# A selective scan on one core: its units ordered by channel half, one PSUM accumulator, and a third PSUM slot for the preparing steps alone

## What is computed

```python
xz = LN(x) @ in_w.T                      # only layer 0 normalizes
xr, z = split(xz)
xc = silu(causal_conv4(xr) + cb)
dt, Bm, Cm = split(xc @ xw.T)            # ranks 8, 16, 16
dt = softplus(dt @ dtw.T + dtb)
dA  = exp(dt[..., None] * A)             # (b, t, 256, 16)
dBx = dt[..., None] * Bm[:, :, None, :] * xc[..., None]
h_t = dA_t * h_{t-1} + dBx_t;   y_t = sum_s h_t[:, s] * C_t[s]
out = ((y + xc * D) * silu(z)) @ ow.T
```

## Time and profile before

| | us |
|---|---|
| median of 3 runs (lowest to highest) | 6413.47 (6411.19 to 6418.31) |
| the profiled execution, its own time | 6412.89 |
| its span | 6411.1 |
| span of the scan block, first instruction to the last DVE operation | 1285.1 |
| first scan of unit 0 starts | 89.00 |
| granted TensorE clock, mean of the span | 0.939 |

### The profile page before, as it was taken

One profiled execution on the slowest core, in us unless ns is written; L12 is line 12 of the kernel. 1 busy time (PEld: TensorE's weight loads), 2 busy tenths in 40 slices (PEclk: granted clock), 3 DMA queues, 4 the chain that ended last, 5 costly groups with the idle time before them and its releaser, 6 DMA issues. The chain is left out here.

```text
span 6411.1 us, 72562 instructions
## 1 busy us (share of the span) xinstructions
PE 5480.3 (85%) x25739; PEld 2272.5 (35%) x25776; DVE 4251.4 (66%) x4740; ACT 2491.3 (39%) x2863; POOL 2457.2 (38%) x1151
## 2 busy tenths in 40 slices
PE   5777777749999999999999999937888776777999
PEld 2333333323333334433343343313333211222776
DVE  3676667867776777677767767547666888773221
ACT  4444444213222323232232222223555566666332
POOL 3666666716655565556555555500000000000000
PEclk8988998979999999999999999967999899998999
DMA  2222222211111101011101101011111101000000
GB/s 81 86 97 86 86 93 93 95 38 28 30 25 25 29 19 39 21 28 25 40 19 25 30 22 25 20 38 45 38 37 31 31 21 24 18 11 28 1 1 14
DMA packets 114962, 247.35 MB, mean 39 GB/s; under 512 B 27564, under 2 KB 48308, under 8 KB 114324
## 3 DMA queue, kind: packets, MB, share of 16 engines
q1 hardware_dynamic: 114616, 242.71, 13.4%
HBM read 200.81 MB, written 23.86 MB: 35 GB/s over the span
## 5 line engine op out<-in xcount | busy, mean ns | idle before, releaser
L2097 DVE TENSOR_REDUCE n_MX<-ps 128x2 f32<-128x1024 f32 (+1 forms) x896 | 979.1, 1108 | 289.0 <-PE ps L1860 206.6
L1547 POOL TENSOR_TENSOR s_PA<-s_PA,s_TMP 128x1024 f32<-128x1024 f32 x384 | 906.5, 2361 | 321.7 <-ACT s_TMP L1268 293.3
L1969 ACT ACTIVATE n_P<-ps 128x1024 f32<-128x1024 f32 (+2 forms) x896 | 804.7, 936 | 462.3 <-PE ps L1878 240.9
L1268 ACT ACTIVATE s_TMP<-ps 128x1024 f32<-128x1024 f32 x512 | 523.9, 1025 | 1145.8 <-PE ps L1128 1133.9
L673 POOL TENSOR_TENSOR m_PR<-m_HH,m_CS 128x1024 f32<-128x1024 f32 x256 | 604.7, 2374 | 395.5 <-DVE m_HH L635 164.9
L1399 DVE TENSOR_REDUCE s_MX<-ps 128x2 f32<-128x1024 f32 x512 | 593.1, 1201 | 17.1 <-PE ps L1111 16.6
L1391 DVE TENSOR_TENSOR XTB<-ps,s_GVJ 128x1024 f32<-128x1024 f32 x256 | 312.9, 1222 | 401.5 <-PE ps L1102 399.1
L1124 PE MATMUL ps<-s_QF 64*128 64x512 f32 x2048 | 554.8, 618 | 10.7 <-DMA s_M<-s_MS 8.4
L472 PE MATMUL ps<-m_PR,ident 128*128 128x512 f32 x1024 | 540.8, 662 | 11.8 <-POOL m_PR L673 11.1
L1904 PE MATMUL ps<-n_P,n_VA 128*32 128x512 f32 (+3 forms) x3584 | 523.1, 582 | 12.2 <-ACT n_P L1969 12.2
L1111 PE MATMUL ps<-s_QF 64*128 64x512 f32 x2048 | 497.9, 603 | 32.9 <-DVE XTB L1391 30.6
(11 more groups left out here) (309 smaller groups left out, 7418.6 us busy)
## 6 DMA issues: line engine op xcount, KB each, us to landing
m_CS<-m_rows_c SPq DMA_DIRECT2D x128, 512.0 KB, 3.9
m_BS<-m_rows_c SPq DMA_DIRECT2D x80, 512.0 KB, 4.8
s_WV<-in_s_v SPq DMA_DIRECT2D x32, 512.0 KB, 3.5
s_TA<-XTB SPq DMA_DIRECT2D x256, 64.0 KB, 2.3
s_WO<-in_s_o SPq DMA_DIRECT2D x32, 512.0 KB, 3.9
n_parts<-n_PT SPq DMA_DIRECT2D x16, 768.0 KB, 3.3
n_QS<-n_parts SPq DMA_DIRECT2D x192, 64.0 KB
n_KS<-n_parts SPq DMA_DIRECT2D x192, 64.0 KB
```

Of the source, the lines that this page charges most:

```text
L1268: s.activation(self.P[g % 4], ps, ACT.Exp).then_inc(*r.take(step))
L1547: g.tensor_tensor(PA, PA, P, ALU.add).then_inc(self.add_done, 1)
L1969: s.activation(self.P[(32 * n + 8 * hp + t) % 3][q][:, :, lo:512], ps.rearrange("p (h n) -> p h n", h=2)[:, :, lo:512], ACT.Exp, scale=sca ...
L2097: v.tensor_reduce(self.MX[:, q, :, hp, t], ps.rearrange("p (h n) -> p h n", h=2)[:, :, 0:width], AX.X, ALU.max).then_inc(*r.take(step))
```

## The change

1. A unit is now `h = m // 16 % 2`, `j = m % 16`: 16 units of half 0, then 16 of half 1. Each unit loads its own C row (`c_in` 256 times instead of 128).
2. There is one accumulator, `PY` (two banks). The first `sum` of a half waits until the half before it is gated. So `gate(n, 0)` stands behind unit 18 and `gate(n, 1)` behind unit 2 of the next item.
3. The two banks that come free are slot 2, which only the side steps use. Units keep slots 0 and 1.
4. Side steps stand at written-out places (`sides`), and the reader's part of a step is a step of its own (`..._t`), one unit or so behind its PE part. The two long `in` are cut in halves (`in0`, `in`) with unit steps between. `dt`, `ln` and `soft` of half 1 are made in the item itself (units 5 to 8) and those of half 0 in the item before (22 to 26); `ln` is done half by half.
5. `make(m + 1)` now comes before `exp(m + 3)`; C is asked for 3 units ahead, B 5. `m_PR` has four tiles instead of three; DT and U have one copy, not two; `m_T` is its own tile.
6. The statistics of all four sequences' layernorms are taken in the first stretch (`stats`, `others`), and later `norm` is only the 8 scalings. The weights for the first matmuls are loaded first, and PE waits for each weight only where it uses it.

```diff
-        self.PY = [PS[:, 0:1024], PS[:, 1024:2048]]
-        self.r = Ring(nc, ctx, "m_psum", [PS[:, 2048:3072], PS[:, 3072:4096]],
+        self.PY = PS[:, 0:1024]
+        self.r = Ring(nc, ctx, "m_psum", [PS[:, 1024:2048], PS[:, 2048:3072], PS[:, 3072:4096]],
...
+    SIDE = 2
+    def sides(self, n):
+        at = {}
+        if n > 0:
+            at[2] = [("gate", n - 1, 1)]
+            at[3], at[4] = [("post", n - 1)], [("post_t", n - 1)]
+        at[5], at[6] = [("dt", n, 1)], [("dt_t", n, 1), ("ln", n, 1)]
+        at[7], at[8] = [("soft", n, 1)], [("soft_t", n, 1)]
+        at[18] = [("gate", n, 0)]
+        if n + 1 < len(self.items):
+            x = n + 1
+            if self.items[x][1] == 0:
+                at[0], at[1] = [("norm", x)], [("rows", x)]
+                at.setdefault(2, []).append(("rows_t", x))
+            at[9], at[10], at[11] = [("in0", x, 0)], [("in", x, 0)], [("in_t", x, 0)]
+            at[12], at[13], at[14] = [("in0", x, 1)], [("in", x, 1)], [("in_t", x, 1)]
+            at[15], at[16] = [("in", x, 2)], [("in_t", x, 2)]
+            at[17] = [("in", x, 3)]
+            at[18] += [("in_t", x, 3), ("silu", x, 0), ("silu", x, 1)]
+            at[20], at[21] = [("bc", x)], [("bc_t", x), ("c_out", x)]
+            at[22], at[23] = [("bc_mid", x), ("bc_res", x), ("dt", x, 0)], [("bc_lo", x)]
+            at[24] = [("dt_t", x, 0), ("ln", x, 0)]
+            at[25], at[26] = [("soft", x, 0)], [("soft_t", x, 0)]
+        return at
...
             for i in range(units):
                 m = units * n + i
-                if m % 2 == 0:
-                    spread(m // 2 + 2)
-                exp(m + 3)
-                early(m + 2)
-                make(m + 1)
+                c_in(m + 3)
+                b_in(m + 5)
+                make(m + 1)
+                exp(m + 3)
+                pmult(m + 2)
                 if not self.by_pool(m):
                     out.append(("mult", m))
                 out.extend([("scan", m), ("prod", m)])
                 if m >= self.LAG:
                     out.append(("sum", m - self.LAG))
-                if n > 0 and i in (1, 2):
-                    out.append(("gate", n - 1, i - 1))
-                if n > 0 and i == 4:
-                    put([("post", n - 1)], m % 2)
-                if i >= 6 and i % 2 == 0 or i in (9, 15, 21):
-                    put(next(side, []), m % 2)
+                for step in sides.get(i, []):
+                    put(step, self.SIDE)
...
+    def unit(self, m):
+        return m // (2 * self.NS), m // self.NS % 2, m % self.NS
...
                 if j == 0:
-                    if item > 0:
-                        pe.wait_ge(self.gated, 2 * (item - 1) + h + 1)
+                    pe.wait_ge(self.dd_done, 4)
+                    if n > 0:
+                        pe.wait_ge(self.gated, 2 * item + h)
```

More of the change, by code:

```diff
@@ L232, in __init__ @@
         self.ZS = [sb(f"ZS{u}", [128, 2, L]) for u in range(2)]
[L233 removed]
+        self.DT = sb("DT", [128, 2, L])
         self.RW = sb("RW", [128, L])
@@ L280, with first @@
+    def first(self):
+        return [(("norm", 0), None), (("rows", 0), 2), (("rows_t", 0), None), (("others", 0), None), (("setup", 0), None),
[3 rows of a table added]
+                (("silu", 0, 1), None), (("bc_t", 0), None), (("c_out", 0), None), (("dt", 0, 0), 2), (("dt_t", 0, 0), None),
+                (("bc_mid", 0), None), (("bc_res", 0), None), (("ln", 0, 0), None), (("bc_lo", 0), None),
+                (("soft", 0, 0), 0), (("soft_t", 0, 0), None)]
     IN_PSUM = ("rows", "in", "bc", "dt", "soft", "post", "dbx")
@@ L284, in order, with put, c_in, b_in @@
         total = N * units
[L286 to L294, removed]
+        def put(step, slot):
+            if step[0] in self.IN_PSUM:
+                place[step] = slot
+            out.append(step)
+        def c_in(m):
+            if m < total:
+                out.append(("c_in", m))
+        def b_in(m):
+            if m < total and self.by_pool(m):
+                out.append(("b_in", m))
+        def pmult(m):
+            if m < total and self.by_pool(m):
+                out.append(("pmult", m))
         def make(m):
@@ L306, in exp @@
                 out.append(("exp", m))
[L308 to L311, removed]
+        for step, slot in self.first():
+            put(step, slot)
+        for m in range(3):
+            c_in(m)
+        for m in range(5):
+            b_in(m)
         for m in range(3):
             exp(m)
-        early(1)
+        pmult(1)
         make(0)
         for n in range(N):
-            side = iter(list(self.before(n + 1)) if n + 1 < N else [])
+            sides = self.sides(n)
             for i in range(units):
                 m = units * n + i
-                if m % 2 == 0:
-                    spread(m // 2 + 2)
+                c_in(m + 3)
+                b_in(m + 5)
+                make(m + 1)
                 exp(m + 3)
-                early(m + 2)
-                make(m + 1)
+                pmult(m + 2)
                 if not self.by_pool(m):
@@ L351, in last_read, with last_units @@
         return "dbx", 2 * self.NS * (item + 1) - 1
+    def last_units(self, item, h):
+        end = 2 * self.NS * item + self.NS * (h + 1)
+        units = range(end - self.NS, end)
+        return ([m for m in units if not self.by_pool(m)][-1], [m for m in units if self.by_pool(m)][-1],
+                sum(self.by_pool(m) for m in range(end)))
     def xt(self, b):
@@ L558, in scalar @@
             elif kind == "ln":
-                s.wait_ge(self.exp_e, 2 * (n + 1))
-                for h in range(2):
-                    s.activation(self.E[h], self.E[h], ACT.Ln, bias=1.0).then_inc(self.ln_done, 1)
-            elif kind == "soft":
                 h = step[2]
-                r.filled(s, step)
+                s.wait_ge(self.exp_e, 2 * n + h + 1)
+                s.activation(self.E[h], self.E[h], ACT.Ln, bias=1.0).then_inc(self.ln_done, 1)
+            elif kind == "soft_t":
+                h, fill = step[2], ("soft", n, step[2])
+                r.filled(s, fill)
+                if n > 0:
+                    kept, in_psum, _ = self.last_units(n - 1, h)
+                    s.wait_ge(self.exp_done, self.exps[kept])
+                    r.filled(s, self.slot(in_psum))
                 s.wait_ge(self.u_done, 2 * n + h + 1)
-                s.activation(self.DT[n % 2][:, h, :], ps, ACT.Copy).then_inc(*r.take(step))
+                s.activation(self.DT[:, h, :], r.ap(fill), ACT.Copy).then_inc(*r.take(fill))
             elif kind == "exp":
-                h, j, item = n % 2, n // 2 % self.NS, n // 2 // self.NS
+                item, h, j = self.unit(n)
                 l = self.items[item][1]
@@ L577, in scalar @@
                         r.taken(s, self.slot(n - 4))
[L578 removed]
+                    s.activation(self.DA[n % 4][:, :], self.DT[:, h, :], ACT.Exp,
                                  scale=scale).then_inc(self.exp_done, 1)
[L580 to L582 removed]
+            elif kind == "post_t" and self.items[n][1] == 0:
+                fill = "post", n
+                r.filled(s, fill)
+                s.activation(self.xt(self.items[n][0])[:, 3:L + 3], r.ap(fill), ACT.Copy).then_inc(*r.take(fill))
         c.own_count_a = own.n
```

247 lines of the change are left out of this document (142 added, 105 removed), and 3 rows, old and new, of the table x.

## The result

The changed kernel takes **6226.65 us** in the median of 4 runs (6221.85 to 6231.07), the one before 6414.7 on the same chip: a ratio of 0.9707, 95% interval 0.969 to 0.9723. The forecast was 6218, range 6140 to 6305. The profiled execution has a span of 6228.4 us.

A forecast was written before the change was run, and what follows sets the result against it. No engine was full: DVE set the undisturbed pace and side steps added some 50 us per item. Seven items -178, last item +3, first stretch -20 gave -195 on 6412.89: 6218 us, range 6140 to 6305.

The forecast's parts named there:

- units 5 to 17: DVE waits for dbx 17, which PE's queue of side passes delivers at 46.5 instead of 37.5: 9.2 us per item.
- gate of half 0: At unit 18 PE's opening, sum and make take 3.9 us against DVE's one pool scan of 2.2: wait 1.7.
- `bc`: At units 20 and 21 DVE's subtraction waits for PE's end and three ACT copies: 3.7 us per item.
- `soft` of half 0: At units 25 and 26 ACT's chain of 5.7 us makes DVE wait 2.2 per item.
- gate of half 1 and `post`: At units 2 and 3 PE's opening, sums, `post` and make take 9.0 us against DVE's 5.7: wait 3.3.
- clock, spread over the item: The 55 us of passes where PE paces run at 0.94 granted clock, costing 3.5 us more per item.
- DVE's own work, 104.8: Per item, 97.5 us of mults and scans for 32 units plus 7.3 for six side operations between scans.
- A sign of being wrong: In the scan block, the forecast is wrong if a wait at a gate exceeds 4 us.
- The norm: Three items preparing a `norm` pay 8 short DVE operations, 2.3 us each item; statistics and square root leave the loop.
- The last item: Loses one gate and a `post` wait, gains waits at units 3, 18 and 8: +3 us on 103.6.
- The first stretch: Before the first scan, earlier root and `in` and a shorter half 0 chain: scan at 69 for 89.00, -20 us.
- L609: DVE's subtraction with two SBUF operands beside POOL: costed at nothing, at most 15 us if all seven were caught.

The follow-up runs named there:

- oldstart: Changed kernel with the earlier start: PE and POOL wait for all weights and constants, ACT makes its constants before the first square root; 6233.85 us, ratio 0.9714.
- shared: Changed kernel with each long `in` whole, all readers at their PE part's place, side steps in the units' slots (m % 2); 6393.49 us, ratio 0.9961.
- whole: Changed kernel with each long `in` again one piece of 8 matmuls instead of two halves in neighbouring units; 6236.62 us, ratio 0.972.

## Why the prediction was right

The predicted median is 8.65 us under the measured one. The forecast started from a profiled execution, and against the changed kernel's (6230.2 us) it is 12 short: 11 in the first seven items, 5 in the last one, less 4 in the blocks that neither kernel differs in, so a quarter of the shortfall was made good by luck. By its steps, for an item without a norm (third item, intervals between scans in DVE's timeline less DVE's own work):

| step | forecast | measured |
|---|---|---|
| first scan | 69 | 69.05 |
| units 5 to 17 | 9.2 | 2.4 + 1.0 + 2.2 + 1.7 + 2.2 = 9.5 |
| gate of half 0 | 1.7 | 7.3 - 3.4 = 3.9 |
| `bc` | 3.7 | 3.4 |
| `soft` of half 0 | 2.2 | 2.4 |
| gate of half 1 and `post` | 3.3 | 9.0 - 3.4 = 5.6 |
| clock, spread over the item | 3.5 | 1.7 + 1.7, both in the gates' rows |
| item | 128.4 | 129.6 |

- **DVE's own work, 104.8**, and PE's price list held: the intervals are 4.4 and 5.6 us where two halves of `in` stand, and there is no long wait for ACT's exps. The 9.2 for units 5 to 17 is more than its own terms give: 11.3 + 34.8 = 46.1, less 37.5, is 8.6.
- **The clock** had the right size and the wrong place. I spread it evenly over 55 us of passes, 3.5 us an item. In the third item what it costs stands at the two gates, 1.7 us each (2.38 + 4.91 for 1.96 + 3.60 at the one, 3.58 + 2.00 for 1.95 + 1.88 at the other, to 0.1). The gates cost 3.9 and 5.6 for 1.7 and 3.3, together 4.5 more: 3.4 is the clock, and 1.1 was missing from the waits. That two sums of passes at 0.94 and two low stretches at gates come to the same 3.5 is chance. Moving the gates brought 61 us where I expected 27 to 47, since it took 3.4 of order and 1.7 of clock at the one gate, and 2.2 and 1.7 at the other.
- **A sign of being wrong** came true: the wait at the gate of half 1 is 5.5 us, and I had said none over 4. The longest waits were to stand at units 9 to 16 and at 21; they stand at the gates. The item's length held because the excess there was the clock that I had put elsewhere.
- **The norm** was mis-sized: 2.3 forecast, 4.2 measured in each of the three items. (Items 3 and 4 are only 3.6 longer than the others, since their gates differ: 10.2 for 9.0, and 5.6 for 7.3.) The eight scalings take 4.24 us between units (in the first stretch, without POOL's products, they take 2.14):

```profile
457.40 4.24 DVE L684 TENSOR_SCALAR m_XN<-X,m_mv,m_rs 128x128 f32<-128x128 f32 x8
...
L684 DVE TENSOR_SCALAR m_XN<-X,m_mv,m_rs x32: 322/336/2412, 9.7 to 594.5; 128x128 f32<-128x128 f32 x32
```

  Their median is 336 ns and the slowest took 2412, so I read the row as seven at the usual price and one that waits 2 us. Operand and result are in SBUF, and POOL is at work; no run takes POOL away there, so that cause is argued and not shown.
- **The last item** is +8, not +3: its two gates cost 9.9 - 3.4 = 6.5 and 8.6 - 3.4 = 5.2, again more than 3.3 and 1.7. Nothing else fills PE there, and the granted clock of its window is 0.92.
- **The first stretch** was right in its sum and not in its parts. The square root ran at 8.43, since its table was loaded before the variance was there; `in` had to wait for the tap products and began at 18.09 instead of 17.5, inside the bound of 19.7. `oldstart` prices this part at 9.7 us by the profile.
- **POOL** was idle before its products for 243.6 us in all, 30 per item, and the trace shows no wait of it for a load of `m_CS`, both as forecast; DMA moved 168 GB/s where I had said 170.
- **L609** (now L699) stayed at a cost of nothing for DVE. It is POOL's product that is long, 3.33 us, beside each of the seven that stand in the units; in the third item:

```profile
420.53 1.22 DVE L699 TENSOR_TENSOR m_T<-m_T,m_BC 64x1024 f32<-64x1024 f32 x1
...
420.63 3.33 POOL L763 TENSOR_TENSOR m_PR<-m_HH,m_CS 128x1024 f32<-128x1024 f32 x1 [4.48 <-issue]
```

  The Trainium skill (SBUF — State Buffer, "SBUF: two separate sides") says so of a DVE operation with two SBUF inputs and a POOL operation: the later one waits for the whole of the earlier. This row agrees: the product starts 0.10 us behind L699 and takes 3.33 for a median of 2.36. On POOL, idle for 4.48 us before it, the wait was covered. I had looked for it only on DVE.

What the forecast did not hold apart is what carries the gain. It named the slot that a long `in` holds; the runs show slot and late readers to be one thing (from `shared` down, the slot alone is worth 20 us, the late readers with DVE's part alone nothing, the slot and all late readers together 157, to `whole`).

## What to carry to other kernels

Give steps that prepare the next item a buffer of their own, and then let each engine's read of it stand a unit behind the fill in that engine's queue: neither helps without the other. In an in-order queue the price of a step is the time that its engine stands still with ready work behind it, so count that for each engine, the vector engine first. Where one accumulator is handed on, put its last read as early as its data allow, so that the engine that reads it has ready work left while the next engine refills it. Here that also took away most of the stretches at the lower clock behind the hand-over.

## What was not expected of the hardware

- TensorE's lower level in short stretches inside a busy block: behind 2.73 us without work some passes took 0.85 us instead of 0.43 (granted clock 0.68 from 337 to 341). The same idle time is not always followed by one: 2.76 us in the third item was (4 records in 3.58 us), 2.75 in the fourth was not (1.95).
- DVE's 128x128 scalings from SBUF to SBUF, 336 ns in the median, took up to 2412 ns beside POOL's products (the cause is argued); the scans and mults of kept units, which have an operand in PSUM, show no such thing in their means (2287 and 1216 ns over 176 each).
- Broadcast loads of 512 KB at 232 GB/s, the DMA engines 0.68 busy, beside all engines at work, without a measurable effect on them.
